# A MetaFormer block on one Trainium2 core: first stage with small loads between x's chunks, tokens normalised by three engines, and attention's weights loaded by head group on GpSimd's queue

## The reference, cut to what matters

```python
x = x + codano(_ln_c(x))          # _ln_c: layer norm of every image row (128 values), eps 1e-6
t = _to_tokens(x)
t = t + ffn(_ln_t(t))             # Wx, batch norm over all rows, then a recurrence
                                  # yt = sigmoid(wx_t + yt @ V.T), step by step
def codano(x):
    tokens = x.reshape(b * t, 1, H, W)
    tokens_norm = instance_norm(tokens)
    k = fno_layer(tokens_norm, key_w, ..., (H//2, W//2))    # spectral conv of low modes + 1x1 skip
    q = fno_layer(tokens_norm, query_w, ..., (H//2, W//2))
    v = fno_layer(tokens_norm, value_w, ..., (H, W))        # 16 heads
    dprod = softmax(einsum('bhtd,bhsd->bhts', qf, kf) / scale)
    attn = einsum('bhts,bhsd->bhtd', dprod, vf)
    attn = fno_layer(attn, proj_w, ..., (H, W))
    attn = instance_norm(attn + tokens)
    m = fno_layer(instance_norm(attn), mixer_w1, ..., act=gelu)
    m = fno_layer(m, mixer_w2, ...)
    return instance_norm(m) + attn
```

## Time and profile before

| | |
|---|---|
| median of 3 runs | 431.83 us |
| lowest, highest | 427.73, 433.30 us |
| span of the profiled execution | 424.2 us, 7190 instructions |
| the profiled execution's own device time | not given; the three runs lie 3.5 to 9.1 us above the span |
| busy: TensorE (PE), VectorE (DVE) | 349.7 us (82%), 338.0 us (80%) |
| busy: ScalarE (ACT), GpSimd (POOL) | 229.5 us (54%), 213.0 us (50%) |
| DMA | 59.42 MB, mean 140 GB/s |

### The profile page before, as it was taken

The page is one execution under the profiler, slowest core; times in us unless marked ns, Lnnn a source line. Parts: engine busy times, 40 slices in busy tenths (PEclk is TensorE's granted clock), DMA queues, the critical chain, the costliest instruction groups (busy, mean ns, idle before and its releaser), DMA issues.

```text
span 424.2 us, 7190 instructions
## 1 busy us (share of the span) xinstructions
PE 349.7 (82%) x2415; PEld 273.7 (65%) x2415; DVE 338.0 (80%) x995; ACT 229.5 (54%) x511; POOL 213.0 (50%) x261
## 2 busy tenths in 40 slices
PE   0289979997794899998999778878888789999950
PEld 0289965974352899987988748634454446767950
DVE  2999762766896967469999686999999759899991
ACT  0498851801023388545655125767886789899000
POOL 1389960000002699399892107887886579900000
PEclk9999999999998699999999969899999999999995
DMA  8999998999805000089799880142232500000998
GB/s 215 249 291 319 288 284 191 220 218 379 339 0 199 2 0 2 2 100 116 91 174 119 100 99 2 46 156 100 101 103 107 192 2 0 2 0 0 276 287 234
DMA packets 62999, 59.42 MB, mean 140 GB/s; under 512 B 5792, under 2 KB 55376, under 8 KB 60912
## 3 DMA queue, kind: packets, MB, share of 16 engines
q1 hardware_dynamic: 43232, 50.24, 40.0%
q0 software_dynamic: 16512, 8.39, 16.2%
q10 hardware_dynamic: 3216, 0.30, 0.7%
HBM read 38.84 MB, written 16.94 MB: 131 GB/s over the span
## 4 chain that ended last, share of the span: by engine, by line
DVE 34%; PE 32%; POOL 12%; DMA 6%; issue 5%; SPq 4%; ACT 4%; DVEq 0%; POOLq 0%; ACTq 0%
PE PS L632 30%; POOL BIG L569 8%; DVE SML L1196 6%; DVE BIG L1337 5%; DVE BIG L1529 4%; DVE BIG L1546 3%; SPq L511 3%; DMA BIG<-in_x 3%; DVE BIG L1613 3%; POOL BIG L588 2%; DMA BIG<-BIG 2%; PE PS L636 2%; DMA BIG<-xn_rows 2%; DVE BIG L1429 1%; DVE BIG L1425 1%
## 5 line engine op out<-in xcount | busy, mean ns | idle before, releaser
L632 PE MATMUL PS<-CST,BIG 128*128 128x128 f32 (+6 forms) x994 | 123.0, 312 | 13.1 <-ACT BIG L1004 4.5
L632 PEld LDWEIGHTS PS<-CST,BIG 128*128 128x128 f32 (+1 forms) x994 | 110.2, 193 | 28.8 <-DVE BIG L1529 8.3
L582 POOL COPY BIG<-BIG 128x512 f32<-128x512 f32 x24 | 29.9, 1291 | 79.2 <-DMA BIG<-xn_rows 75.3
L632 PE MATMUL PS<-BIG 128*128 128x128 f32 (+2 forms) x450 | 53.8, 368 | 5.9 <-DVE BIG L1337 5.4
L1196 DVE BATCH_NORM_STATS2 SML<-BIG 128x6 f32<-128x128 f32 x256 | 53.5, 279 | 5.8 <-DMA BIG<-in_x 4.4
L636 PEld LDWEIGHTS PS<-CST,BIG 128*128 128x128 f32 (+1 forms) x326 | 41.6, 183 | 19.5 <-issue 12.4
L632 PEld LDWEIGHTS PS<-BIG 128*128 128x128 f32 (+2 forms) x450 | 40.6, 168 | 16.7 <-issue 8.7
L636 PE MATMUL PS<-CST,BIG 128*128 128x128 f32 (+1 forms) x326 | 49.0, 291 | 2.5 <-ACT SML L400 1.4
L632 PE MATMUL PS<-BIG,SML 128*128 128x256 f32 (+4 forms) x230 | 48.8, 415 | 0.0
L400 ACT ACTIVATE BIG<-PS 128x512 f32<-128x512 f32 (+3 forms) x59 | 32.2, 569 | 26.0 <-PE PS L632 21.0
L569 POOL TENSOR_SCALAR BIG<-BIG,SML 128x128 f32<-128x128 f32 x84 | 40.3, 498 | 9.0 <-DVE SML L1216 9.0
(11 more groups left out here) (218 smaller groups left out, 487.3 us busy)
## 6 DMA issues: line engine op xcount, KB each, us to landing
xn_rows<-BIG SPq DMA_DIRECT2D x8, 1024.0 KB, 9.4
BIG<-xn_rows SPq DMA_DIRECT2D x8, 1024.0 KB, 9.2
BIG<-in_x POOLq DMA_DIRECT2D x8, 1024.0 KB, 11.0
BIG<-rs_rows SPq DMA_DIRECT2D x8, 1024.0 KB, 4.7
out_x<-BIG SPq DMA_DIRECT2D x32, 256.0 KB, 3.6
BIG<-wy_rows SPq DMA_DIRECT2D x16, 192.0 KB, 5.8
BIG<-BIG SPq DMA_DIRECT2D x16, 192.0 KB, 8.0
BIG<-in_L_conv_mixer_w SPq DMA_DIRECT2D x2, 544.0 KB, 9.1
```

The source lines that it names most:

```text
L582: pool.tensor_copy(x_mix[:, g % MIX_RING], columns(g)).then_inc(S("x_mix_pool"), 1)
L632: return pe.matmul(o, l, rhs, start=start, stop=stop, **k)
```

## The change

Five edits, which belong together: (1) the 17 small loads are issued by SP, three behind each of x's chunks 2 to 7; (2) `LN_BY` gives each group of four tokens to an engine: 72 tokens to GpSimd, 44 to ScalarE, 12 to VectorE, and three copies of spectra (n = 27, 29, 31) go to VectorE, ahead of its projection weights; the row variances come before these too, s1 before `mqk`; (3) `rx`, `wr`, `u` and the products lie elsewhere in BIG2, so that `rx` needs chunks 0 and 1 written, `wr` 2 to 4, `u` 5 to 7; (4) ScalarE alone does the 8 moves of `rx`; (5) `wr` is loaded from GpSimd's queue, the 4 heads of group 0 first, the other 12 behind `rep_x_01`, and each group has its own semaphore; the loops of the 16 copies of `ts` are exchanged and their partitions rotated.

```diff
-LN_POOL = [8, 8, 12, 12, 12, 12, 12, 8]
+LN_BY = ["PPAA", "PPAA", "PPAA", "PPPA", "PPPA", "PPPA", "PPDA", "PDDA"]
...
+P1_AT = [4 * c + k for c in range(XC) for by in "ADP" for k in range(4) if LN_BY[c][k] == by]
...
+RS_DVE = (27, 29, 31)
...
-XN_OUT = 4 * ["xn_0_3"] + 2 * ["xn_4_5"] + 2 * ["xn_6_7"]
+XN_OUT = 2 * ["xn_0_1"] + 3 * ["xn_2_4"] + 3 * ["xn_5_7"]
...
-        rx = BIG2[:, 8192:12288].rearrange("f (j t) -> f j t", t=NT)
+        rx = BIG2[:, 0:4096].rearrange("f (j t) -> f j t", t=NT)
...
-        wr = BIG2[:, 0:6144].rearrange("p (g w k h) -> p g w k h", g=4, k=3, h=MH)
+        wr = BIG2[:, 4096:10240].rearrange("p (g w k h) -> p g w k h", g=4, k=3, h=MH)
...
                 sp.dma_start(x_h[:, tokens, :], x_row[:, tokens, :]).then_inc(S(f"x_in{c}"), 16)
+                if c >= 2:
+                    for name, a, k in small[3 * c - 6:3 * c - 3]:
+                        sp.dma_start(PRM[:, a:a + k], flat(t[name]).to_broadcast([128, k])).then_inc(S("prm"), 16)
...
-            sp.wait_ge(S("wy_out"), 16)
-            sp.wait_ge(S("rs_filled"), 48 // P1_T)
-            sp.wait_ge(S("xn_0_3"), 64)
-            for n in range(NH):
-                sp.dma_start(wr[TB * (n % HG):TB * (n % HG) + TB, n // HG].rearrange("s w k h -> s (w k h)"),
-                             wy_rows[n:n + 1, :].to_broadcast([TB, 3 * MW * MH])).then_inc(S("rep_w"), 16)
...
-            for b in range(NB):
-                for n in range(HG):
+            for k in range(HG):
+                for b in range(NB):
+                    n = (b + k) % HG
                     sp.dma_start(xrep[TB * n:TB * n + TB, b].rearrange("s w k h -> s (w k h)"),
...
@@ gpsimd, behind its normalisations
+            def head_rows(n):
+
+                pool.dma_start(wr[TB * (n % HG):TB * (n % HG) + TB, n // HG].rearrange("s w k h -> s (w k h)"),
+                               wy_rows[n:n + 1, :].to_broadcast([TB, 3 * MW * MH])).then_inc(S(f"rep_w{n // HG}"), 16)
+
+            pool.wait_ge(S("wy_out"), 16)
+            pool.wait_ge(S("rs_filled"), 80 // P1_T)
+            pool.wait_ge(S("xn_2_4"), 48)
+            for n in range(HG):
+                head_rows(n)
+            pool.wait_ge(S("rep_x_01"), 32 * HG)
+            for n in range(HG, NH):
+                head_rows(n)
...
@@ scalar
             spectra(XC - 1)
             root(s("s1"), s("rt"))
-            act.wait_ge(S("xn_4_5"), 32)
-            empty(act, "rx", 0, 8, move_rx)
+            act.wait_ge(S("xn_0_1"), 32)
+            for n in range(8):
+                act.wait_ge(S("rx_filled"), n + 1)
+                move_rx(act, n).then_inc(S("rx"), 1)
...
@@ vector
             for c in range(XC):
                 if c + 1 < XC:
                     dve.wait_ge(S(f"x_in{c + 1}"), 16)
                     ln_moments(c + 1, x_h, range(XR), row_var)
+                if c:
+                    normalise(c - 1)
                 ln_coefs(c, "ln_coef")
+            normalise(XC - 1)
+            link(TT(row_var, row_var, ln_r, ALU.mult))
+            TT(row_var, row_var, ln_r, ALU.mult).then_inc(S("vr"), 1)
+            for n in RS_DVE:
+                dve.wait_ge(S("rs_filled"), n + 1)
+                move_rs(dve, n).then_inc(S("rs_dve"), 1)
...
-            dve.wait_ge(S("xn_4_5"), 32)
-            empty(dve, "rx", 0, 8, move_rx)
...
+                if hg:
+                    dve.wait_ge(S(f"rep_w{hg}"), 16 * HG)
...
-            dve.wait_ge(S("rep_w"), 16 * NH)
+            dve.wait_ge(S("rep_w0"), 16 * HG)
```

More of the change, by code:

```diff
@@ L54, with ln_done @@
 P1_N = NT // P1_T
[L56 to L58 removed]
+P1_AT = [4 * c + k for c in range(XC) for by in "ADP" for k in range(4) if LN_BY[c][k] == by]
+P1_BY = "".join(LN_BY)
+def ln_done(by, c):
+    return P1_BY[:4 * c].count(by)
+RS_DVE = (27, 29, 31)
 LAG_P2, LAG_M2 = 5, 7
 MIX_RING = 5
[L61 removed]
+XN_OUT = 2 * ["xn_0_1"] + 3 * ["xn_2_4"] + 3 * ["xn_5_7"]
 MIX_ACT = 4
@@ L489, in _ @@
             sp.dma_start(CST[:, 0:n], t["const"][:, 0:n]).then_inc(S("basis_in"), 16)
+            small = [(name, a, k) for name, (a, k) in ROW_AT.items() if k <= NH]
             for c in range(XC):
@@ L567, in _ @@
                 pool.wait_ge(S("ln_coef"), c + 1)
[L568 to L571, removed]
+                for k in range(4):
+                    if LN_BY[c][k] == "P":
+                        for n in range(XR * c + 4 * k, XR * c + 4 * k + 4):
+                            last = pool.tensor_scalar(x_h[:, n, :], x_h[:, n, :], ln_r[:, n:n + 1],
+                                                      ln_b[:, n:n + 1], ALU.mult, ALU.add)
                         last.then_inc(S("ln_pool"), 1)
             pool.memset(gf, 0.0).then_inc(S("gf_zero"), 1)
+            def head_rows(n):
[9 more added lines that the diff above has]
+                head_rows(n)
             pool.wait_ge(S("prod"), 2 * NH)
@@ L636, in tr, with rs_kept @@
                 return pe.matmul(o, i, ident[0:n, 0:n], is_transpose=True, start=True, stop=True)
+            def rs_kept(pe, n):
+                if k := sum(m < n for m in RS_DVE):
+                    pe.wait_ge(S("rs_dve"), k)
+                pe.wait_ge(S("rs"), n - k)
             def gram(b, q0, q1):
@@ L656, in _ @@
                 for n in range(4 * c, 4 * c + 4):
[L657 to L661, removed]
+                    by = P1_BY[P1_AT[n]]
+                    done = P1_BY[:P1_AT[n] + 1].count(by)
+                    pe.wait_ge(S({"A": "ln_act", "P": "ln_pool", "D": "ln_dve"}[by]), done)
                     if n >= 4:
-                        pe.wait_ge(S("rs"), n - 3)
+                        rs_kept(pe, n - 3)
                     for j in range(P1_T):
@@ L1002, in _ @@
                 act.wait_ge(S("ln_coef"), c + 1)
[L1003 to L1006, removed]
+                for k in range(4):
+                    if LN_BY[c][k] == "A":
+                        for n in range(XR * c + 4 * k, XR * c + 4 * k + 4):
+                            last = act.activation(x_h[:, n, :], x_h[:, n, :], ACT.Identity,
+                                                  scale=ln_r[:, n:n + 1], bias=ln_b[:, n:n + 1])
                         last.then_inc(S("ln_act"), 1)
@@ L1230, in _, with normalise @@
             TS(w_t, w_t, s("wm"), None, ALU.subtract).then_inc(S("w_centred"), 1)
+            def normalise(c):
+                for k in range(4):
+                    if LN_BY[c][k] == "D":
+                        for n in range(XR * c + 4 * k, XR * c + 4 * k + 4):
+                            last = TS(x_h[:, n, :], x_h[:, n, :], ln_r[:, n:n + 1], ln_b[:, n:n + 1],
+                                      ALU.mult, ALU.add)
+                        last.then_inc(S("ln_dve"), 1)
             for c in range(XC):
```

48 lines of the change are left out of this document (22 added, 26 removed).

## The result

| | time, us (lowest to highest), runs | ratio to the kernel before |
|---|---|---|
| before | 429.8 (425.2 to 433.3), 6 | |
| changed | 438.0 (431.3 to 441.6), 6 | 1.018 [1.012, 1.023] |

The changed kernel is slower by 1.8%: 7.6 us by the ratio, 8.2 between the medians. The forecast was no change (432.1, range 427.5 to 439.0). The time lies inside the range and the difference within 2%, but the interval does not hold 1: a small loss is there, and the forecast sum, +0.3 us, missed it.

What follows compares the result with a forecast made beforehand. It took TensorE, without a gap, to be as late as GpSimd. Earlier spectra -0.8, uncovered weights and root +5.0, shorter DMA queue -3.9 gave +0.3 on 431.8: 432.1 us, range 427.5 to 439.0.

Steps and rivals of the forecast that it cites:

- the forecast sum, +0.3 us: Whole kernel: -0.8 for the spectra's end, +5.0 for weights and root uncovered, -3.9 for a shorter queue.
- four signs of being wrong: Weights done before 62; ts before 76 or after 80; first products waiting for copies beyond 97.5; group 1 stopping VectorE.
- a rival that came in another form: Attention's weight loads: slow issue by GpSimd makes group 1 late; 441 in all, chance 0.14, half of it inside the range.
- stall of TensorE at 30 us, then pace: Spectra, chunk 2: TensorE waits 1.35 us for ScalarE's late copies of chunk 1, then keeps 5.36 us per chunk.
- the bound that the chain made of it: Normalisations up to 60 us: rival with GpSimd as the bound, relief of 9.8 us, 422.0; chance 0.04.
- The weights' lost cover: Projection weights on VectorE, now behind the last spectra: price 7.5 us, between 6.5 and 8.5.
- Cold TensorE: Gram matmuls after a stand of some 5 us: rival with clock at 1.2 GHz, +1.7 to +3.5 us, chance 0.14.
- a shorter DMA queue: Copies of ts: only 4 of 16 weight loads go ahead, so copies start into an empty queue; -3.9 us.
- weights by head group, no wait: Attention's weights: group 1 lands at 105.3, before its products at 107.1; groups 2 and 3 have 9 us more each.
- the rival's "+4.6": Group 1's weights: landing at 111.7 if each issue costs GpSimd 2.6 us, delay of 4.6; late-weights chance 0.14.
- small loads, 0: Start of the kernel: 17 small loads on SP between x's chunks fit into idle waiting; taken as 0, bound +2.5.

Runs made afterwards that it cites:

- g3: Changed kernel with ScalarE doing all 32 spectra copies, eight weight loads before the wait, and chunk 2's third token group given to GpSimd; 424.2 us, 0.986.
- e1: Changed kernel with RS_DVE empty: ScalarE does all 32 copies of spectra, VectorE goes straight to the projection weights; 428.5 us, 0.997.
- e2: Changed kernel with ten matmuls on constants into an unused bank while TensorE waits for the first rx move; 434.6 us, 1.013.
- f1: Changed kernel with RS_DVE empty and eight weight loads (groups 0 and 1) issued before the wait for rep_x_01; 424.6 us, 0.991.
- f2: Changed kernel with RS_DVE empty and SP's reload of the tokens held back until group 1's weights have landed; 424.5 us, 0.995.
- f3: Changed kernel with five matmuls on constants into an unused bank while TensorE waits for the first rx move; 432.2 us, 1.016.
- g2: Kernel before with only the small loads moved to SP's queue, between x's chunks; 433.2 us, 1.011.
- e3: Changed kernel without GpSimd's wait for rep_x_01 ahead of the last twelve weight loads; 436.0 us, 1.013.
- f4: Kernel before with the queue edit alone: weights by head group on GpSimd's queue, exchanged order of the copies of ts; 430.2 us, 1.008.

## Why the prediction was off, inside its range

By its own steps, at the operation that each step names:

The number lies inside the range partly by luck. Three of the four signs of being wrong that the prediction set itself came: `ts` after 80, the first products waiting for copies beyond 97.5 (99.86), and group 1 stopping VectorE. The time is 6 us from the forecast, outside its 2.5 us, and the range reached to 439.0 for a rival that came in another form: several costs, each of them a rival of its own or put at nothing, added up.

| step | forecast | measured |
|---|---|---|
| stall of TensorE at 30 us, then pace | 1.35; 5.36 | 1.41; 5.36 |
| last spectra filled, last copy by VectorE | 60.3 | copy from 59.99 |
| GpSimd's last normalisation ends | before 55 | 52.7 |
| weights, L1293 to L1312 | 7.5 | 7.2 |
| first rx move | 69.2 | 68.33 |
| mode matmuls | 74.05 | 76.39 |
| `ts` | 78.25 | 80.58 |
| `rep_x_01` in | 95.5 | 99.8 |
| products of batches 2 and 3 | 99.3 | 103.33 |
| group 1's weights | no wait | wait of 3.61 |

**Right.** GpSimd was not the bound that the chain made of it: 7.3 us came off it (52.7 for 60.0) and nothing behind it moved by as much. But TensorE had waited 1.7 us for it, and the new stall of 1.41 takes most of that back: the matmul behind the last spectra starts at 61.04 before, 59.78 in the changed kernel, and 58.03 in g3, without the stall. TensorE without a gap decided, and e1 shows the whole gain (`ts` 1.4 us earlier). The weights' lost cover was named, its term priced within 0.3 us (7.2 for 7.5), and e1 shows that this one edit carries the loss, with what follows from it. The four operations of L1299 took 0.37 us each with GpSimd idle; beside it, as L1255, 443 ns. So the term came out a little below what I took, not at its lower end of 6.5. By the Trainium skill's page "SBUF — State Buffer", section "SBUF: two separate sides", the two take turns at a port pair; these rows agree with it. ScalarE, idle too at that time in the changed kernel, isn't the cause: in e1 it works beside L1299 (53.0 to 55.6 us), as TensorE does, GpSimd has ended, and L1299 takes 0.37 to 0.39 us.

**The step on the clock.** "Cold TensorE" was a rival at 0.14 and came true, inside its price of 1.7 to 3.5 us: 7.08 us for 4.08, 3.0. At the mode matmuls 2.3 of it is left (76.39 - 74.05), since the first rx move came 0.9 earlier than forecast. The forecast took the gap as free of a clock change while the earlier trace rows already showed one around a gap of 5.76 us. It came a second time at 120 us, behind the wait for group 1 (a gap of 4.2 us; granted clock 0.56 over 120 to 127 us), which cost another 1.9 us between group 1 and group 2 (11.39 us; in e2, with the clock at 1.00 there, 9.52). That one stood in no sum, since no wait at group 1 was foreseen.

**The step "a shorter DMA queue", -3.9 us.** 2.2 us of it held: the products of batches 2 and 3 start 22.75 us behind `ts`, before 24.96. What is missing is the first products' wait of 1.96 us for `rep_x_01`, 16.2 us behind the first issue for 14.2 forecast. I had the fourteenth copy land in proportion to its place in the queue. By 95 us 2.3 MB had been moved (7 us at 172 GB/s and 5 at 224, by the windows above), of 2.75 MB in fourteen copies. The small rest needed 4.8 us more; the last two copies and the mixer's loads were then in flight beside it, which is the likely cause but wasn't tried alone. e1, f1, f2 and f3 show the same wait, 1.55 to 1.85 us.

**The step "weights by head group, no wait".** The rival gave this step a price through GpSimd's issue, 1.45 us or more. Issue was cheap, 0.49 us (median), half of what I took, and as cheap beside VectorE's products as before them; what the prediction cited for the rival, descriptors that GpSimd can't write, didn't show. What was mis-sized is the landing: 5.8 us was read from a stretch of before with no bulk reload beside the loads. Here group 1's loads go out at 100 us beside the mixer's loads and the reload of 1 MB pieces, and take 13.2. f2 shows that as the cause. The result, +3.6, is the rival's "+4.6" by another mechanism.

**The step "small loads, 0".** VectorE's waits were all that I looked at, and the loads don't fit into idle waiting: a chunk of x costs SP 0.72 us for 3.30, but the small load behind it then takes up to 3.62. SP's queue has work of its own behind x, and reaches it 3 us later. g2 prices this at 1.011 [1.005, 1.017] in the kernel before; that it costs the changed kernel anything isn't shown.

**The sum again**, up to L1423: +4.3 at batches 2 and 3 (forecast +0.3), the difference of 4.0 being 3.0 for the clock, less 0.7 as the moves began early, and 2.0 for the copies, less 0.3 by smaller terms; +3.6 at group 1; +1.9 for the second cold spell; together 9.8 of the 9.9 us. The time over all moved by 7.6. What lies between isn't settled. Part of the 9.9 may belong to this one execution: in f3 the wait for group 1 is 2.79 us and the second spell costs 1.0 (10.49 us to group 2), 1.7 less together. And half-clock spells of TensorE in later stages come and go between executions: from 150 to 420 us the windows add up to 14 us at 1.2 GHz in f3, 18 before, 27 in the changed kernel and 37 in g3.

## What to carry to other kernels

The engine in the chain that ended last is the bound only if no other is as late: look for a second one without a gap before pricing its relief. Work that waits for nobody is cover for others; put ahead of it one wait that blocks, and it moves to the path with everything queued behind it, on other engines too, and the gap may cost a clock spell on top. A landing time read from a quiet stretch doesn't hold when the transfer is issued later, beside a bulk load; hold the bulk load back instead, if it has time.

## What was not expected of the hardware

- Loads of 192 KB on GpSimd's queue cost it 0.49 us each to issue (0.73 at most), beside VectorE's products too.
- Transfers of 192 KB into 32 partitions ran at 216 to 240 GB/s with no bulk reload beside them, from either queue and in either order (before 216 to 221 from 76 to 95 us; f2 221 and 227 from 95 to 105), while the stretch 99 to 106 us of before, reload included, ran at 422. With the loads mixed into the reload in the changed kernel, everything together got 380 from 100 to 105 us, but only 238 to 259 from 105 to 127.
- In the changed kernel, gaps of TensorE of 4.2 and 4.6 us each went with about 6.8 us at 1.2 GHz; in e3 the gap of 4.6 went with only 3.3. The gaps ahead of group 1's matmuls in e1 (3.44 us) and f3 (3.34) had such a spell behind them, the one in e2 (2.16) none. Five matmuls in the gap at 64 us kept it at 2.4 GHz. But a gap isn't the only thing that brings one on: f4 has a spell with only gaps up to 0.66 us ahead of it.
- In g2 the issue of a small load mostly takes 0.43 us (0.75 at most), but 1.57 to 3.62 us when it is the first behind a chunk of x; the hold moves from the chunk to whatever follows it.
